# Two cross-attentions in one kernel: TensorE transposes the probabilities of two steps ago before, not after, it computes the new scores

## The chip, the cores and the metric

The kernel runs on one core of one Trainium2 chip. The metric is device time in microseconds (us) of one execution, smaller being better.

## The reference

A stack of four layers on a residual stream `x` (2 x 256 rows, 512 wide) with a context `ctx` (2 x 512 rows, 512 wide). Each layer is a cross-attention and a feed-forward part, each with its own gate:

```
x = x + tanh(g_xattn[0]) * L0_xattn(layernorm(x), ctx)
x = x + tanh(g_ffn[0])   * L0_ffn(layernorm(x))
x = x + tanh(g_xattn[1]) * L1_xattn(layernorm(x), ctx)
x = x + tanh(g_ffn[1])   * L1_ffn(layernorm(x))
...                          # layers 2 and 3: other attentions and MLPs
```

The first two attentions are the ones that the change touches. Both are grouped-query attentions whose keys and values come from the context followed by the rows themselves (512 + 256 = 768 keys for each of the 2 batches):

```
hidden = concat([ctx, x_normed])                 # 768 keys
q = x_normed @ Wq ; k = hidden @ Wk ; v = hidden @ Wv
attn = softmax(q k^T / sqrt(head_dim)) ; out = (attn v) @ Wo
# L0: 32 heads, 4 key/value heads, head_dim 128;  L1: 16 heads, 4 key/value heads, head_dim 96
```

## The kernel before, in words

One program with five engine streams, written by hand and held together by semaphores. The functions `att_pe`, `att_act`, `att_dve`, `att_pool` and `att_sp` are called once for each of the first two attentions (`A0`, then `A1`). A trip `it` runs over the 4 key/value heads, so `head(it, ...)` is executed 4 times for `A0` and 4 times for `A1`: 8 trips in all. Inside a trip the queries of all heads of the group are cut into items of 128 rows: 4 items a head, so 32 items a trip in `A0` (8 heads) and 16 in `A1` (4 heads).

A trip is a software pipeline over steps `n` (items + 4 of them). In step `n` the engines do, each in its own program order:

- TensorE (PE): the scores of item `n` (L611, 6 matmuls: queries times 768 keys, in a high and a low part of each factor), into banks 0-1 or 2-3 by the parity of `n`; now and then an output product `inner` (L576, 3 matmuls); the turn, that is the transposing of the probabilities of item `m = n - 2` (L625, 6 transposes), into banks 4 and 5; half of a product of probabilities and values of the items four and three back (L637, 9 matmuls); and a last job `job` in bank 7: a query projection of a later head ("Q", L569, 12 matmuls) or an output product of an earlier one ("O", L576, 3 matmuls).
- VectorE (DVE): the row maxima of item `n` (L813); the add of an `inner` output product (L763); every fourth step a reciprocal (L819); the remainder of the turned probabilities of item `n - 2` (L824: what the rounded copy leaves of them, read from banks 4 and 5); in odd steps the remainder of an output (L830); in steps with n % 4 = 1 a piece of the quantising of later weights (L778 to L800); the add or remainder of the `job` (L763, L767).
- ScalarE (ACT): the rounded copy of the turned probabilities of item `n - 2` (L715, read from banks 4 and 5), then the exponentials of item `n` (L722), in odd steps an output copy (L728), and the copy of a query projection (L693).

The jobs follow a fixed table (`A.steps`): a Q in steps 1, 5, 9, ... while heads are left; an O in steps 6, 7 and 8 of the first head, 10, 11 and 12 of the second, and so on, with the head's fourth O as `inner` in step 9, 13, ... Steps 2 to 4 have no job. So in the middle of a trip one step in four (n % 4 = 1) is long, with an inner O and a Q, and three are short, with one O each.

What the turn waits for: `exps` of its own item (`m + 1`), and `pT` of the item before (`m`), which DVE counts up when L824 has read banks 4 and 5, since there is one pair of banks for the turned probabilities. What the scores wait for: `exps` of item `n - 2`, whose banks they overwrite. GpSimd (POOL) splits weights into parts and SyncE (SP) issues the loads; neither is named in the change.

Of the kernel before, what the change touches and what calls it, by code (L numbers as in the profile page):

```python
# [21 lines left out]
P = 128  # L22
# [7 lines left out]
VT = S // P  # L30
# [100 lines left out]
def build(nc, t, out):  # L131
    with ExitStack() as ctx:
        sems = {}

        def sem(name):
            if name not in sems:
                sems[name] = ctx.enter_context(nc.semaphore(name))
            return sems[name]

        def sb(name, shape, dt=F32, scope=ctx):  # L140
            return scope.enter_context(nc.sbuf_tensor(name, shape, dt))

        ps = ctx.enter_context(nc.psum_tensor("ps", [P, 8, 512], F32))
# [3 lines left out]
        def bank(b, n=512, p=P):  # L147
            return ps[0:p, b, 0:n]


        ident = sb("ident", [P, P])
# [19 lines left out]
        with ExitStack() as grp:  # L171
# [7 lines left out]
            prob = sb("prob", [P, 3, S], F32, grp)  # L179
            pT = sb("pT", [P, 2, 2, VT, ROWS // B], F32R, grp)  # L180
# [246 lines left out]
        def credits(engine, name, A):  # L427
            for n, by in credit.items():
                if by == name and A is A0:
                    engine.sem_inc(sem(f"att_{n}"), 1)  # L430
# [109 lines left out]
        def att_pe(pe, A, u):  # L540
            s = {n: sem(f"att_{n}") for n in att_per(A)}
            hd = A.hd
            credits(pe, "tensor", A)
            def project(w, it, c, b):

                for k in range(KT):
                    for wp, xp in PAIRS:
                        rhs = ctxT[:, xp, k, c * CTX:(c + 1) * CTX] if c < B else xT[:, xp, k, :]
                        last = nc.tensor.matmul(bank(b, 512, hd), wkv[:, w, wp, k * hd:(k + 1) * hd], rhs,  # L549
                                                start=(k == 0 and (wp, xp) == PAIRS[0]),  # L550
                                                stop=(k == KT - 1 and (wp, xp) == PAIRS[-1]))
                last.then_inc(s["kv_full"], 1)

            def keys(it, c):
                if c == 0:
                    pe.wait_ge(s["split"], at(it, A, "split", 1))
                    pe.wait_ge(s["kv"], at(it, A, "kv", 0))
                project(0, it, c, c)

            def work(it, job, b=7):  # L560
                kind, h, r = job
                if b == 7:

                    pe.wait_ge(s["w"], at(it, A, "w", A.place[job] - 1))
                if kind == "Q":
                    pe.wait_ge(s["split"], at(it, A, "split", A.split["q", h]))
                    for k in range(KT):
                        for wp, xp in PAIRS:
                            last = nc.tensor.matmul(bank(b, 512, hd), wq[:, h % 2, wp, k * hd:(k + 1) * hd],  # L569
                                                    xT[:, xp, k, :], start=(k == 0 and (wp, xp) == PAIRS[0]),  # L570
                                                    stop=(k == KT - 1 and (wp, xp) == PAIRS[-1]))
                else:
                    pe.wait_ge(s["split"], at(it, A, "split", A.split["o", h]))
                    pe.wait_ge(s["oT"], at(it, A, "oT", 2 * h + r // 2 + 1))
                    for op, wp in PAIRS:
                        last = nc.tensor.matmul(bank(b), oT[0:hd, h % 2, op, r * P:(r + 1) * P],  # L576
                                                wo[0:hd, h % 2, wp, :], start=(op, wp) == PAIRS[0],
                                                stop=(op, wp) == PAIRS[-1])
                last.then_inc(s["w_full"], 1)

            def values(it):

                pe.wait_ge(s["split"], at(it, A, "split", 2))
                for c in range(3):
                    pe.wait_ge(s["kv"], at(it, A, "kv", c + 1))
                    project(1, it, c, c)
                work(it, ("Q", 0, 0))

                for c in range(3):
                    pe.wait_ge(s["kv_hi"], at(it, A, "kv_hi", 3 + c + 1))  # L590
                    for j in range(4):
                        last = nc.tensor.transpose(ps[:, 4 + c, j * hd:(j + 1) * hd],
                                                   vturn[0:hd, c, j * P:(j + 1) * P], ident[0:hd, 0:hd])
                    last.then_inc(s["kv_full"], 1)

            def head(it, ahead):
                def wait(name, n):
                    pe.wait_ge(s[name], at(it, A, name, n))

                for n, inner, job in A.steps:  # L600
                    if n < A.items:
                        h, r = divmod(n, RT)
                        b = r // 2
                        if r == 0:
                            wait("w", A.place["Q", h, 0])
                        if n >= 2:
                            wait("exps", n - 1)
                        sc = ps[:, 2 * (n % 2):2 * (n % 2) + 2, :].rearrange("p a c -> p (a c)")
                        for lo, hi in ((0, 512), (512, S)):
                            for qp, kp in PAIRS:  # L610
                                last = nc.tensor.matmul(sc[:, lo:hi], qT[0:hd, h % 2, qp, r * P:(r + 1) * P],  # L611
                                                        kT[0:hd, kp, b, lo:hi], start=(qp, kp) == PAIRS[0],
                                                        stop=(qp, kp) == PAIRS[-1])
                        last.then_inc(s["scores"], 1)
                    if inner:
                        work(it, inner)
                    if 2 <= n < A.items + 2:
                        m = n - 2
                        wait("exps", m + 1)
                        if m == 0:  # L620
                            wait("kv", 6)
                        if m >= 1:
                            wait("pT", m)
                        for j in range(VT):
                            last = nc.tensor.transpose(ps[:, 4 + j // 3, (j % 3) * P:(j % 3 + 1) * P],  # L625
                                                       prob[:, m % 3, j * P:(j + 1) * P], ident[:])
                        last.then_inc(s["turned"], 1)
                    if n >= 4:
                        q, second = divmod(n - 4, 2)
                        b = q % B  # L630
                        if not second:
                            wait("pT", 2 * q + 2)
                            if q >= 1:
                                wait("oT", q)
                        for j in range(3 * second, 3 * second + 3):
                            for vp, pp in PAIRS:
                                last = nc.tensor.matmul(bank(6, 256, hd), vv[:, vp, b * VT + j, 0:hd],  # L637
                                                        pT[:, q % 2, pp, j, :],
                                                        start=(j == 0 and (vp, pp) == PAIRS[0]),
                                                        stop=(j == VT - 1 and (vp, pp) == PAIRS[-1]))  # L640
                        if second:
                            last.then_inc(s["pv"], 1)
                    if job:
                        work(it, job)
                    if ahead and A.items <= n < A.items + 3:
                        keys(it + 1, n - A.items)
                for job in A.tail:
                    work(it, job, TAIL_BANKS[job[2]])
                if ahead:
                    values(it + 1)  # L650

            if A is A0:
                pe.wait_ge(sem("ctx_split"), 1)
                keys(0, 0)
                turn_pe(pe, u)
                pe.wait_ge(sem("ctx_split"), 2)
                keys(0, 1)
            else:
                keys(0, 0)
                keys(0, 1)  # L660
                turn_pe(pe, u)
            pe.wait_ge(sem("xT_lo"), (u // 2 + 1) * RT)
            keys(0, 2)
            values(0)
            with pe.Fori(0, A.kv - 1) as it:
                head(it, True)
            head(A.kv - 1, False)

        def kv_dst(A, part, c):
# [1372 lines left out]
```

## Time and profile before

| | |
|---|---|
| three runs | 1490.13, 1492.81, 1494.40 us; median 1492.81 |
| the profiled execution | 1491.04 us in all, span of its instructions 1489.3 us |
| mean granted TensorE clock | 0.969 of full speed |
| busy share of the span | PE 92%, weight loads of PE 72%, DVE 65%, ACT 40%, POOL 31% |

The profile's span goes from the first instruction to the last; 1.7 us of the execution lie outside. The first attention's steps lie between about 44 and 650 us of the span, the second's between about 730 and 1060 us. In the profile a group of matmuls is shown with the time of its first start; the start of the next group on the same engine says how long it kept the engine.

### The profile page before, as it was taken

What the parts mean: (1) busy time and instruction counts of PE and PEld (TensorE: products, weight loads), DVE (VectorE), ACT (ScalarE), POOL (GpSimd) and SP (SyncE); (2) the same over time, 40 slices, a digit from 0 to 9 for tenths busy, and PEclk for the clock granted to TensorE, in tenths of its full rate; (3) what the DMA queues carried; (4) which work ended last, traced back from release to release, by engine and by line L of the source; (5) the groups of instructions that cost most, each with busy time, mean ns of one, the idle gap of its engine ahead of it and who ended that gap; (6) DMA issues with size and microseconds to landing.
All of it is one profiled execution on the core that took longest, in us unless ns stands there. A gap on an engine that the chain in (4) does not pass through costs nothing.

```text
span 1489.3 us, 22423 instructions
## 1 busy us (share of the span) xinstructions
PE 1369.5 (92%) x8021; PEld 1073.0 (72%) x8027; DVE 965.4 (65%) x1394; ACT 599.4 (40%) x1037; POOL 467.3 (31%) x357
## 2 busy tenths in 40 slices
PE   5999989998999999989899999999689999899765
PEld 4898879887889888854687887878665444577422
DVE  3778657874878478853584865746655773463697
ACT  2544434443444344420443534434325677122111
POOL 2361445153434334421242243530232002144100
PEclk9999999999999999999999999999888999999878
DMA  5210112011110211021002011110230000561000
GB/s 184 57 40 22 61 45 61 28 61 44 36 47 22 68 57 47 8 78 37 27 1 65 21 53 32 32 38 9 72 96 1 1 2 1 139 163 44 0 0 29
DMA packets 54335, 68.13 MB, mean 46 GB/s; under 512 B 26416, under 2 KB 34896, under 8 KB 54240
## 3 DMA queue, kind: packets, MB, share of 16 engines
q1 hardware_dynamic: 54240, 66.84, 14.9%
q8 instruction: 62, 1.02, 0.3%
q14 instruction: 33, 0.27, 0.1%
HBM read 57.13 MB, written 5.37 MB: 42 GB/s over the span
## 4 chain that ended last, share of the span: by engine, by line
PE 80%; DVE 12%; issue 3%; ACT 3%; DMA 1%; POOL 0%; SPq 0%; DVEq 0%; POOLq 0%; ACTq 0%
PE ps L637 12%; PE ps L611 11%; PE ps L549 9%; PE ps L625 9%; PE ps L576 8%; PE ps L569 8%; PE ps L1502 4%; PE ps L1133 3%; PE ps L1159 3%; PE ps L1515 2%; DVE pT L824 2%; PE ps L1115 1%; ACT pT L715 1%; PE ps L1144 1%; PE ps L882 1%
## 5 line engine op out<-in xcount | busy, mean ns | idle before, releaser
L715 ACT ACTIVATE pT<-ps 128x768 fp32r<-128x768 f32 x192 | 156.0, 812 | 291.8 <-PE ps L625 291.8
L637 PE MATMUL ps<-pT,vv 128*128 128x256 f32 (+1 forms) x1728 | 249.7, 289 | 2.5 <-DVE oT L830 2.5
L824 DVE TENSOR_TENSOR pT<-ps,pT 128x768 fp32r<-128x768 f32 x192 | 183.7, 957 | 92.9 <-ACT pT L715 92.5
L611 PE MATMUL ps<-kT,qT 128*128 128x512 f32 (+3 forms) x1152 | 233.0, 339 | 4.0 <-DVE qT L767 2.6
L611 PEld LDWEIGHTS ps<-kT,qT 128*128 128x128 f32 (+1 forms) x1152 | 198.9, 188 | 43.5 <-DVE qT L767 4.2
L637 PEld LDWEIGHTS ps<-pT,vv 128*128 128x128 f32 (+1 forms) x1728 | 215.5, 180 | 4.3 <-DVE pT L824 2.9
L813 DVE TENSOR_REDUCE nmax<-ps 128x1 f32<-128x768 f32 x192 | 182.2, 951 | 23.0 <-PE ps L611 20.1
L722 ACT ACTIVATE prob<-ps,nmax 128x768 f32<-128x768 f32 x192 | 172.2, 897 | 30.2 <-DVE nmax L813 30.0
L625 PE MATMUL ps<-ident,prob 128*128 128x128 f32 x1152 | 158.7, 274 | 19.2 <-DVE pT L824 19.2
L576 PE MATMUL ps<-wo,oT 128*128 128x512 f32 (+1 forms) x576 | 163.5, 399 | 4.3 <-DVE qT L767 2.6
L625 PEld LDWEIGHTS ps<-ident,prob 128*128 128x128 f32 x1152 | 130.8, 140 | 31.6 <-ACT prob L722 17.8
L763 DVE SCALAR_TENSOR_TENSOR x<-ps,rden,x 128x512 f32<-128x512 f32 x192 | 143.2, 746 | 7.5 <-PE ps L576 2.6
L569 PE MATMUL ps<-xT,wq 128*128 128x512 f32 (+1 forms) x576 | 142.1, 395 | 0.0
L529 POOL TENSOR_TENSOR wo<-raw,one 128x512 fp32r<-128x512 f32 (+1 forms) x48 | 50.0, 1041 | 275.1 <-PE ps L576 275.1
L529 POOL TENSOR_TENSOR wq<-raw,one 128x512 fp32r<-128x512 f32 (+1 forms) x48 | 46.6, 971 | 255.9 <-PE ps L569 141.5
L569 PEld LDWEIGHTS ps<-xT,wq 128*128 128x128 f32 (+1 forms) x576 | 100.6, 179 | 27.0
L549 PE MATMUL ps<-ctxT,wkv 128*128 128x512 f32 (+1 forms) x384 | 95.0, 401 | 16.6 <-POOL wkv L532 15.0
L576 PEld LDWEIGHTS ps<-wo,oT 128*128 128x128 f32 (+1 forms) x576 | 97.0, 189 | 17.0 <-POOL wq L532 2.7
L1348 DVE TENSOR_REDUCE qrow<-ps 128x1 f32<-128x512 f32 x128 | 83.3, 687 | 36.9 <-PE ps L1133 35.7
L767 DVE SCALAR_TENSOR_TENSOR qT<-ps,qT 128x512 fp32r<-128x512 f32 (+1 forms) x48 | 33.0, 687 | 103.1 <-ACT qT L693 101.8
L1442 POOL TENSOR_TENSOR f2w<-f2raw,f2w 128x1024 fp32r<-128x1024 f32 (+1 forms) x22 | 43.1, 1963 | 178.5 <-ACT f2w L1546 177.4
L549 PEld LDWEIGHTS ps<-ctxT,wkv 128*128 128x128 f32 (+1 forms) x384 | 68.2, 179 | 37.8 <-issue 15.5
(224 smaller groups left out, 1869.2 us busy)
## 6 DMA issues: line engine op xcount, KB each, us to landing
f2raw<-in_f_w SPq DMA_DIRECT2D x11, 776.0 KB, 4.5
w3in<-in_m_w SPq DMA_DIRECT2D x11, 768.0 KB, 4.5
raw<-in_l_wq SPq DMA_DIRECT2D x32, 256.0 KB, 2.8
raw<-in_l_wo SPq DMA_DIRECT2D x32, 256.0 KB, 2.6
raw<-in_l_wq SPq DMA_DIRECT2D x16, 192.0 KB, 2.4
raw<-in_l_wo SPq DMA_DIRECT2D x16, 192.0 KB, 2.4
w3gu<-w3o SPq DMA_DIRECT2D x11, 256.0 KB, 2.6
ctxraw<-in_ctxT SPq DMA_DIRECT2D x2, 1024.0 KB, 7.6
```

Of the source, the lines that this page charges most:

```text
L529: nc.gpsimd.tensor_tensor(dst[:, HI], src, one[0:src.shape[0], :].to_broadcast(src.shape), ALU.mult).then_inc(s["split_hi"], 1)
L549: last = nc.tensor.matmul(bank(b, 512, hd), wkv[:, w, wp, k * hd:(k + 1) * hd], rhs, start=(k == 0 and (wp, xp) == PAIRS[0]), stop=(k == K ...
L569: last = nc.tensor.matmul(bank(b, 512, hd), wq[:, h % 2, wp, k * hd:(k + 1) * hd], xT[:, xp, k, :], start=(k == 0 and (wp, xp) == PAIRS[0] ...
L576: last = nc.tensor.matmul(bank(b), oT[0:hd, h % 2, op, r * P:(r + 1) * P], wo[0:hd, h % 2, wp, :], start=(op, wp) == PAIRS[0], stop=(op, w ...
L611: last = nc.tensor.matmul(sc[:, lo:hi], qT[0:hd, h % 2, qp, r * P:(r + 1) * P], kT[0:hd, kp, b, lo:hi], start=(qp, kp) == PAIRS[0], stop=( ...
L625: last = nc.tensor.transpose(ps[:, 4 + j // 3, (j % 3) * P:(j % 3 + 1) * P], prob[:, m % 3, j * P:(j + 1) * P], ident[:])
L637: last = nc.tensor.matmul(bank(6, 256, hd), vv[:, vp, b * VT + j, 0:hd], pT[:, q % 2, pp, j, :], start=(j == 0 and (vp, pp) == PAIRS[0]), ...
L715: nc.scalar.activation(turned_p(m, HI), ps[:, 4:6, 0:S // 2].rearrange("p a (j c) -> p a j c", j=3), ACT.Copy).then_inc(s["pT_hi"], 1)
L722: nc.scalar.activation(prob[:, n % 3, :], sc[:, 0:S], ACT.Exp, bias=nmax[:, n:n + 1], accum_out=rsum[:, n:n + 1]).then_inc(s["exps"], 1)
L763: nc.vector.scalar_tensor_tensor(x[:, r, :], bank(b), rden[:, RT * h + r:RT * h + r + 1], x[:, r, :], ALU.mult, ALU.add).then_inc(s["w"], 1)
L813: nc.vector.tensor_reduce(nmax[:, n:n + 1], sc[:, 0:S], AX.X, ALU.max, negate=True).then_inc(s["nmax"], 1)
L824: nc.vector.tensor_tensor(to, ps[:, 4:6, 0:S // 2].rearrange("p a (j c) -> p a j c", j=3), hi, ALU.subtract).then_inc(s["pT"], 1)
```

## The change

In every step of `head` in `att_pe` the block of the turn (its three waits, its 6 transposes and its semaphore) is moved up, in front of the block of the scores. No instruction is added, removed or changed, and no other engine's program is touched. In a step PE now does: turn of item `n - 2`, scores of item `n`, inner O, product with the values, job.

```diff
                 for n, inner, job in A.steps:
+                    if 2 <= n < A.items + 2:
+                        m = n - 2
+                        wait("exps", m + 1)
+                        if m == 0:
+                            wait("kv", 6)
+                        if m >= 1:
+                            wait("pT", m)
+                        for j in range(VT):
+                            last = nc.tensor.transpose(ps[:, 4 + j // 3, (j % 3) * P:(j % 3 + 1) * P],
+                                                       prob[:, m % 3, j * P:(j + 1) * P], ident[:])
+                        last.then_inc(s["turned"], 1)
                     if n < A.items:
                         h, r = divmod(n, RT)
                         b = r // 2
...
                         last.then_inc(s["scores"], 1)
                     if inner:
                         work(it, inner)
-                    if 2 <= n < A.items + 2:
-                        m = n - 2
-                        wait("exps", m + 1)
-                        if m == 0:
-                            wait("kv", 6)
-                        if m >= 1:
-                            wait("pT", m)
-                        for j in range(VT):
-                            last = nc.tensor.transpose(ps[:, 4 + j // 3, (j % 3) * P:(j % 3 + 1) * P],
-                                                       prob[:, m % 3, j * P:(j + 1) * P], ident[:])
-                        last.then_inc(s["turned"], 1)
                     if n >= 4:
```

## Rows read from the trace of the kernel before

**Rows 1.** The page: busy time, share of the span and instructions of each engine.
```profile
PE 1369.5 (92%) x8021; PEld 1073.0 (72%) x8027; DVE 965.4 (65%) x1394; ACT 599.4 (40%) x1037; POOL 467.3 (31%) x357
```

**Rows 2.** The page: the chain that ended last, share of the span by engine.
```profile
PE 80%; DVE 12%; issue 3%; ACT 3%; DMA 1%; POOL 0%; SPq 0%; DVEq 0%; POOLq 0%; ACTq 0%
```

**Rows 3.** The page: groups, out<-in, count | busy, mean ns | idle before, its ender.
```profile
L824 DVE TENSOR_TENSOR pT<-ps,pT 128x768 fp32r<-128x768 f32 x192 | 183.7, 957 | 92.9 <-ACT pT L715 92.5
...
L763 DVE SCALAR_TENSOR_TENSOR x<-ps,rden,x 128x512 f32<-128x512 f32 x192 | 143.2, 746 | 7.5 <-PE ps L576 2.6
```

**Rows 4.** The waits: who waited for whom, us in total, times, longest.
```profile
PE ps L625 <- DVE pT L824: 19.2, 24, 2.4
```

**Rows 5.** Timeline, two short steps of `A0`: start, duration, engine, line, [idle before].
```profile
228.97 1.21 PE L611 MATMUL ps<-kT,qT 128*128 128x512 f32 x6
...
230.02 0.82 PE L625 MATMUL ps<-ident,prob 128*128 128x128 f32 x6
230.41 0.95 DVE L813 TENSOR_REDUCE nmax<-ps 128x1 f32<-128x768 f32 x1
...
230.59 1.31 PE L637 MATMUL ps<-pT,vv 128*128 128x256 f32 x9
...
231.27 0.17 DVE L819 RECIPROCAL rden<-rsum 128x4 f32<-128x4 f32 x1
...
231.74 0.86 PE L576 MATMUL ps<-wo,oT 128*128 128x512 f32 x3
...
232.44 1.20 PE L611 MATMUL ps<-kT,qT 128*128 128x512 f32 x6
...
233.48 0.93 PE L576 MATMUL ps<-wo,oT 128*128 128x512 f32 x3
233.68 0.96 DVE L813 TENSOR_REDUCE nmax<-ps 128x1 f32<-128x768 f32 x1 [0.29 <-PE ps L611]
```

**Rows 6.** Timeline, steps 2 to 4 of the fourth trip of `A0`, PE and DVE.
```profile
523.58 0.94 DVE L813 TENSOR_REDUCE nmax<-ps 128x1 f32<-128x768 f32 x1
...
524.45 0.94 DVE L824 TENSOR_TENSOR pT<-ps,pT 128x768 fp32r<-128x768 f32 x1
...
525.53 0.85 PE L625 MATMUL ps<-ident,prob 128*128 128x128 f32 x6 [0.98 <-DVE pT L824]
...
526.13 1.29 PE L611 MATMUL ps<-kT,qT 128*128 128x512 f32 x6
...
528.36 0.85 PE L625 MATMUL ps<-ident,prob 128*128 128x128 f32 x6 [0.94 <-DVE pT L824]
...
532.96 2.96 PE L569 MATMUL ps<-xT,wq 128*128 128x512 f32 x12
```

**Rows 7.** Timeline of PE, the last steps of `A0` (29 to 32) in its fourth trip.
```profile
630.54 1.20 PE L611 MATMUL ps<-kT,qT 128*128 128x512 f32 x6
...
634.06 1.21 PE L611 MATMUL ps<-kT,qT 128*128 128x512 f32 x6
...
641.45 0.85 PE L625 MATMUL ps<-ident,prob 128*128 128x128 f32 x6 [0.22 <-DVE pT L824]
```

**Rows 8.** Timeline of PE, two short steps of `A1`.
```profile
840.39 1.20 PE L611 MATMUL ps<-kT,qT 96*128 96x512 f32 x6
...
843.82 1.20 PE L611 MATMUL ps<-kT,qT 96*128 96x512 f32 x6
```

**Rows 9.** Timeline of PE, start of the second trip of `A0`.
```profile
211.75 1.99 PE L611 MATMUL ps<-kT,qT 128*128 128x512 f32 x6
213.97 1.51 PE L625 MATMUL ps<-ident,prob 128*128 128x128 f32 x6 [0.24 <-DVE pT L824]
215.13 1.48 PE L637 MATMUL ps<-pT,vv 128*128 128x256 f32 x9
```

**Rows 10.** Windows: stretch, us and count by engine, granted clock, DMA share, GB/s.
```profile
213.00:216.00 3.00, 2.76 (x16) 2.50 (x15) 1.82 (x3) 1.20 (x3) 0.00 (x0) 0.59 0.03 12
...
652.00:656.00 4.00, 1.99 (x9) 1.31 (x7) 3.79 (x10) 0.00 (x0) 0.73 (x2) 1.00 0.02 4
```

## The prediction

> **What bounds the kernel now.** I read the page first, its busy shares and its chain, then the waits, then the timeline of a few steps. PE is busy for 92% of the span [rows 1] and makes 80% of the chain that ended last [rows 2], so each microsecond that PE loses inside a trip is lost to the end. In the two attentions PE hardly waits: the largest entry that the change touches is the turn (L625) waiting for DVE's remainder of the turn before (L824), 19.2 us in 24 waits [rows 4], that is three for each of the 8 trips: two near its start [rows 6] and one near its end [rows 7]. Everything between runs without a gap. The slack is on the other side: DVE sits idle for 92.5 us in front of L824, waiting for ACT's copy of the turned probabilities [rows 3].
>
> A short step of `A0` takes 3.47 us (scores at 228.97, next scores at 232.44), and that is PE's own work and nothing else: scores 1.05, turn 0.57, product with the values 1.15, output product 0.70 [rows 5]. In `A1` it takes 3.43 us [rows 8].
>
> **What the change does to the order.** PE's program is cyclic, so between one turn and the next it issues the same groups as before, and the work of PE as a sum is unchanged. What changes is what stands between the turn and the scores. There is one pair of banks for the turned probabilities, so turn `m` waits until DVE has done remainder `m - 1`. DVE's own program is not touched: in step `n` it does the maxima of item `n` first, and only then the remainder of item `n - 2`. Before, the scores of step `n` were computed ahead of turn `n - 2`: when the turn was done, DVE was already through the maxima or nearly so. After, the turn comes first, but DVE still can't do its remainder until it has done the maxima of scores that PE only now begins. From turn to turn there is a chain, which after the change goes
>
> turn, scores, maxima, remainder, next turn.
>
> **Its length, link by link.** A turn that had to wait keeps PE for 0.60 us until the next group starts (525.53 to 526.13) [rows 6], one that did not for 0.57 (230.02 to 230.59) [rows 5]. From the start of the scores to the start of the maxima, with DVE waiting for them, 1.24 us (232.44 to 233.68) [rows 5]. From the start of the maxima to the start of the remainder directly behind them 0.87 us (523.58 to 524.45) [rows 6]. The remainder itself takes 0.96 us [rows 3]. From its end to the start of the waiting turn 0.14 us (524.45 + 0.94 = 525.39, turn at 525.53) [rows 6]. Sum: 0.60 + 1.24 + 0.87 + 0.96 + 0.14 = 3.81 us. In a step with n % 4 = 0 the reciprocal stands between maxima and remainder: it takes 0.17 us [rows 5], with its start I count 0.20, so 4.01 us. In the first short step behind a long one the turn has not waited: 3.78 us.
>
> ACT is not in this chain: its copy starts when the turn's 0.6 to 0.85 us are over and is done about 1.7 us behind the turn's start, while the maxima end at 0.60 + 1.24 + 0.87 = 2.71 us. So the 92.5 us of DVE before L824 mostly go away, and reappear as idle time before the maxima (L813), where they are no use.
>
> So the chain is longer than PE's own work in a short step, and PE must wait for the difference in every one of them. In a long step (n % 4 = 1, with a Q of 2.8 us) it is covered: there PE has over 6 us of work of its own. Behind a Q, DVE also has its remainder of the new queries to do before the maxima; the turn now lies between, so this is no later than the scores.
>
> **The sum.**
> - Short steps in threes. Each three of `A0` costs (3.78 - 3.47) + (3.81 - 3.47) + (4.01 - 3.47) = 0.31 + 0.34 + 0.54 = 1.19 us. There are 6 such threes in a trip (steps 6 to 8 up to 26 to 28) and 4 trips: 24 x 1.19 = 28.6. In `A1`, with 3.43: 0.35 + 0.38 + 0.58 = 1.31, 2 threes in a trip: 8 x 1.31 = 10.5.
> - The start of a trip, steps 3 to 5, without output products. Before, from the turn of step 3 to the Q of step 5 it takes 532.96 - 525.53 = 7.43 us, with a wait of 0.94 in it [rows 6]. The turn of step 3 stays where it is: it waits for the remainder of item 0, and DVE comes to that late because of the quantising and the queries' remainder in front of maxima 2, with the turn moved or not. After it come 3.81 (step 3), 4.01 (step 4) and turn, scores and product 0.60 + 1.05 + 1.15 = 2.80: 10.62 us, 3.19 more. 8 trips: 25.5.
> - Step 29 (`A1`: 13), which has an inner output product and no Q. Before: 634.06 - 630.54 = 3.52 [rows 7]. After: DVE has the add of the inner product between maxima and remainder, 0.75 us [rows 3], 0.67 apart with the same overlap of 0.07 as between maxima and remainder. 3.81 + 0.67 = 4.48, so 0.96 more; 8 x 0.96 = 7.7.
> - The last two steps with scores (30, 31). Before, 641.45 - 634.06 = 7.39, with the wait of 0.22 in it [rows 7]; after 2 x 3.81 = 7.62: 0.23 more, 8 x 0.23 = 1.8. Later steps have no scores, and their order doesn't change.
>
> 28.6 + 10.5 + 25.5 + 7.7 + 1.8 = 74.1 us, from 136 steps that the chain sets (23 in a trip of `A0`, 11 in one of `A1`). No DMA, no instruction of another engine is added or moved past another, and SP and POOL are far from the path: later loads only get more time. On the profiled execution's own 1491.0 us this makes 1565.1; the median of the three runs shown is 1.8 us above it, so 1567.
>
> **Bounds of it.** The trace of before has no step in this order, so each link is taken from another place. With the least value of each (0.57 for the turn, 0.94 for the remainder) the chain is 3.76; with no overlap on DVE at all (0.95 for the maxima) 3.89. I take 3.81, as its links are each read where somebody really waited. Minus 0.05 to plus 0.08 over 136 steps is -7 to +11 us; another 0.05 either way on the step from the last score matmul to the maxima, which I have only from places where another group follows the scores, 7 us. The forecast's own range is 1553 to 1585.
>
> One rule of the Trainium skill would size a link otherwise. In the rows two DVE operations start 0.87 us apart where the first is recorded with 0.94 [rows 6]. The page "VectorE: DVE Perf Modes", section "The DRAIN you can't avoid", says that the next operation doesn't start until the pipeline is empty; by that the chain would be at least 0.07 longer, 136 x 0.07 = 10 us and 1577 in all, but here the row contradicts it, and I keep the row.
>
> **The rivals.**
> - *The clock falls at the trips' starts.* After the change PE is idle for about half of steps 3 and 4 (work 1.65 of 3.81, 2.80 of 4.01), and a little in step 5's surroundings. In the second trip of `A0` the granted clock did fall, to 0.59 of full speed over three microseconds [rows 10], after a wait of 2.4 us; scores then take 1.98 us (213.97 - 211.75 less the 0.24 of waiting) in place of 1.05 and the turn 1.16 (215.13 - 213.97) in place of 0.57 [rows 9], 1.5 us more for both. Two such steps in all 8 trips: 24 us, 1591. Against it: three of four trips of `A0` had the same kind of start and kept the clock, and at 652 to 656 us PE was busy half of the time at full clock [rows 10]. Some of it may happen.
> - *It falls all along.* PE would now have a gap of about 0.3 us in every short step. If the clock swung down for a good half of the 136 steps, 70 x 1.5 = 105 us: 1672. Nothing in the rows has such a pattern of small regular gaps; full clock through half-idle stretches speaks against it. By the Trainium skill ("TensorE: Matmul & The Clock Gate", section "A second HAM failure mode: psum-queue depth-cycling") frequent small idle times between groups of matmuls can make the clock gate swing between its two levels; no row here shows it.
> - *Half of the chain is covered.* If DVE starts the maxima earlier than I read, or PE holds less than 3.47 us of work in the new order, and the chain came to 3.6 us, the short steps would cost half, the rest somewhat less: about 74 - 136 x 0.2 = 47 us, 1540. The links are too well seen for this.
> - *No change.* The order is only rotated, PE's sum of work is the same and PE is the bound. This holds if the chain stays under PE's 3.43 to 3.47 us. It needs an error of 0.35 us in five links that sum to 3.81. 1493.
> - *Faster.* The turn comes 1.05 us earlier relative to the scores, ACT's copy too, DVE no longer idles for it (92.5 us), and PE's 19.2 us of waits for L824 [rows 4] go: 1474. It decides for this side if the remainder can be done ahead of the maxima. DVE's program order forbids that.
>
> **Chances.** Forecast 0.76; clock at the starts 0.10; clock all along 0.02; half covered 0.06; no change 0.03; faster 0.03. The range, 1545 to 1592, takes the forecast with its bounds and the case of the starts; outside are the last four and a small part of the first. A measurement can tell about 0.3% (4.5 us) from no change: faster 0.03, same 0.03, slower 0.94.
>
> **What the profile after would show.** Span about 1563, PE's busy time near 1370 and so near 88%. PE L625 waiting for DVE L824 not 24 times but in nearly each short step, 140 to 180 times, 90 us or so in all. In a short step turns 3.8 us apart, 4.0 where the reciprocal stands; in a long step unchanged. L824 directly behind L813 (0.87 apart) with hardly any wait for ACT, and DVE idle before L813 for PE L611 much more than before. At the start of a trip turns at 3.8 and 4.0 and a wait of PE of some 2 us before each. The prediction is wrong in mechanism if L824 still waits for ACT, if the turns are 3.5 us apart, or if the groups of PE themselves become longer at a lower clock.

## The result, and the profile after

The changed kernel takes 1584.52 us (median of 4 runs, 1583.25 to 1587.12), the kernel before 1491.47 us (4 runs, 1488.20 to 1494.40): a ratio of 1.0638, 95% interval 1.0600 to 1.0677. It is 93 us slower. The forecast was 1567 us, in a range of 1545 to 1592; direction and mechanism were right, the size was 74 of 93 us, and the measured time lies in the range, near its upper end.

The page of the changed kernel: busy time by engine, then the chain that ended last by engine, then three of its groups, which answer to [rows 1 to 3].

```profile
PE 1407.3 (89%) x8027; PEld 1066.0 (67%) x8027; DVE 953.0 (60%) x1394; ACT 617.9 (39%) x1037; POOL 467.6 (30%) x357
...
PE 68%; DVE 19%; issue 9%; ACT 2%; DMA 1%; POOL 0%; SPq 0%; DVEq 0%; POOLq 0%; ACTq 0%
...
L813 DVE TENSOR_REDUCE nmax<-ps 128x1 f32<-128x768 f32 x192 | 183.4, 957 | 202.2 <-PE ps L622 199.1
...
L609 PE MATMUL ps<-ident,prob 128*128 128x128 f32 x1152 | 163.5, 279 | 79.9 <-DVE pT L824 62.7
...
L824 DVE TENSOR_TENSOR pT<-ps,pT 128x768 fp32r<-128x768 f32 x192 | 181.2, 944 | 1.9 <-ACT pT L715 1.9
```

The scores are L622 now and the turn L609. PE's part of the chain has fallen from 80 to 68%, DVE's has risen from 12 to 19%. DVE's idle time has moved: the 92.5 us in front of the remainder [rows 3] are 1.9, and in front of the maxima there are 199 us of waiting for scores, where the kernel before had 20.

The waits of PE in the changed kernel (us in total, times, longest), to be read beside [rows 4]:

```profile
PE ps L609 <- DVE pT L824: 62.7, 104, 4.3
PE ps L609 <- ACT prob L722: 17.0, 40, 1.0
```

Together 80 us in 144 waits, against 19.2 in 24. The second row is the same wait as the first: the turn waits for both semaphores, and where the reciprocal stands in the step the profile names the wrong one (the exponentials were long done, the remainder ended 0.15 us ahead of the turn, as the next rows show).

The timeline of three short steps in a row (a "three") in the second trip of the first attention, PE and DVE (the first turn stands behind a long step):

```profile
240.20 0.82 PE L609 MATMUL ps<-ident,prob 128*128 128x128 f32 x6
...
244.07 0.84 PE L609 MATMUL ps<-ident,prob 128*128 128x128 f32 x6 [0.24 <-DVE pT L824]
244.67 1.29 PE L622 MATMUL ps<-kT,qT 128*128 128x512 f32 x6
...
245.80 1.24 PE L637 MATMUL ps<-pT,vv 128*128 128x256 f32 x9
246.00 0.96 DVE L813 TENSOR_REDUCE nmax<-ps 128x1 f32<-128x768 f32 x1 [1.20 <-PE ps L622]
246.88 0.95 DVE L824 TENSOR_TENSOR pT<-ps,pT 128x768 fp32r<-128x768 f32 x1
...
247.97 0.84 PE L609 MATMUL ps<-ident,prob 128*128 128x128 f32 x6 [0.23 <-DVE pT L824]
...
250.86 0.93 DVE L824 TENSOR_TENSOR pT<-ps,pT 128x768 fp32r<-128x768 f32 x1
...
251.94 0.84 PE L609 MATMUL ps<-ident,prob 128*128 128x128 f32 x6 [0.30 <-ACT prob L722]
```

This is the chain of the prediction, and it can be read off link by link between 244.07 and 247.97: turn 0.60, scores to maxima 1.33, maxima to remainder 0.88, remainder 0.95, 0.14 to the next turn; 3.90 us. The turns lie 3.87, 3.90 and 3.97 us apart; the forecast was 3.78, 3.81 and 4.01.

### The profile page after: what moved, and what is told of

It is laid out like the page before. It is cut to its first block, busy times and chain, and to the rows that moved or that the text cites. A ratio compares the mean times of both kernels' runs of the same rounds, so it can differ in the third digit from the quotient of the medians.

```text
span 1581.5 us, 22459 instructions
## 1 busy us (share of the span) xinstructions
PE 1407.3 (89%) x8027; PEld 1066.0 (67%) x8027; DVE 953.0 (60%) x1394; ACT 617.9 (39%) x1037; POOL 467.6 (30%) x357
## 4 chain that ended last, share of the span: by engine, by line
PE 68%; DVE 19%; issue 9%; ACT 2%; DMA 1%; POOL 0%; SPq 0%; DVEq 0%; POOLq 0%; ACTq 0%
PE ps L622 12%; PE ps L609 10%; PE ps L549 8%; PE ps L569 8%; DVE pT L824 6%; PE ps L637 4%; DVE nmax L813 4%; PE ps L1502 4%; PE ps L576 3%; PE ps L1133 2%; PE ps L1159 2%; PE ps L1515 2%; PE ps L1115 1%; PE ps L1144 1%; PE ps L882 1%
## 5 line engine op out<-in xcount | busy, mean ns | idle before, releaser
L813 DVE TENSOR_REDUCE nmax<-ps 128x1 f32<-128x768 f32 x192 | 183.4, 957 | 202.2 <-PE ps L622 199.1
L622 PE MATMUL ps<-kT,qT 128*128 128x512 f32 (+3 forms) x1152 | 251.6, 356 | 3.4 <-DVE qT L767 3.2
L637 PE MATMUL ps<-pT,vv 128*128 128x256 f32 (+1 forms) x1728 | 237.3, 282 | 2.2 <-DVE oT L830 2.1
L609 PE MATMUL ps<-ident,prob 128*128 128x128 f32 x1152 | 163.5, 279 | 79.9 <-DVE pT L824 62.7
L637 PEld LDWEIGHTS ps<-pT,vv 128*128 128x128 f32 (+1 forms) x1728 | 220.7, 182 | 9.4 <-DVE pT L824 2.5
L609 PEld LDWEIGHTS ps<-ident,prob 128*128 128x128 f32 x1152 | 127.5, 142 | 139.4 <-issue 92.9
L622 PEld LDWEIGHTS ps<-kT,qT 128*128 128x128 f32 (+1 forms) x1152 | 192.0, 193 | 30.8 <-DVE qT L767 5.1
L824 DVE TENSOR_TENSOR pT<-ps,pT 128x768 fp32r<-128x768 f32 x192 | 181.2, 944 | 1.9 <-ACT pT L715 1.9
L569 PE MATMUL ps<-xT,wq 128*128 128x512 f32 (+1 forms) x576 | 144.4, 399 | 0.4
L569 PEld LDWEIGHTS ps<-xT,wq 128*128 128x128 f32 (+1 forms) x576 | 100.2, 179 | 32.0 <-issue 4.0
```

The lines of the kernel that those rows point to most:

```text
L813: nc.vector.tensor_reduce(nmax[:, n:n + 1], sc[:, 0:S], AX.X, ALU.max, negate=True).then_inc(s["nmax"], 1)
L824: nc.vector.tensor_tensor(to, ps[:, 4:6, 0:S // 2].rearrange("p a (j c) -> p a j c", j=3), hi, ALU.subtract).then_inc(s["pT"], 1)
```

## The experiments

All runs of a batch shared the chip with runs of the kernel before, whose medians were 1491.42, 1491.30 and 1492.82 us. Turn-to-turn distances below are read from the timeline of PE of each profiled execution.

**e1: VectorE does the remainder first.**

```diff
                 for n, inner, job in A.steps:          # att_dve
+                    if 2 <= n < A.items + 2:
+                        ...                            # the remainder of item n - 2
                     if n < A.items:
                         ...                            # the maxima of item n
```

> The changed kernel, with one thing more: in each step VectorE does the remainder of the turned probabilities (item n-2) before the maxima (item n), so that the remainder no longer waits for scores that come behind the turn. Theory A (the loss is the chain turn, scores, maxima, remainder, next turn): the chain becomes turn, ScalarE copy, remainder, next turn, about 2.85 us, shorter than the 3.48 us of TensorE's own work in a short step; short steps fall from 3.90 back to about 3.48, and the time to 1485 to 1502 us. Theory B (the loss is in TensorE itself: its groups or its clock are worse in the new order, transposes ahead of scores): VectorE's order doesn't matter and the time stays at 1560 us or more.

Measured: 1565.85 us, ratio 1.0511 (1.0479 to 1.0542). Theory A's time was missed by far, and by the time alone theory B (1560 us or more) would have been right. The steps decide against B: the first two short steps of a three are 3.48 and 3.47 us, as A has it, so the chain did go. The loss came back elsewhere. Long steps took 7.74 us in place of 6.58, the third short step 3.84. The waits of PE in e1:

```profile
PE ps L569 <- DVE x L763: 28.4, 24, 1.3
PE ps L609 <- DVE pT L814: 27.8, 23, 2.6
PE ps L637 <- DVE oT L830: 22.7, 33, 1.4
```

The query projection (L569) waits for DVE to empty bank 7, and the product with the values (L637) for the remainder of the output. Neither was in the theory. The timeline of e1 around such a long step:

```profile
250.87 0.85 PE L576 MATMUL ps<-wo,oT 128*128 128x512 f32 x3
251.38 0.96 DVE L814 TENSOR_TENSOR pT<-ps,pT 128x768 fp32r<-128x768 f32 x1 [1.04 <-ACT pT L715]
...
252.26 0.95 DVE L819 TENSOR_REDUCE nmax<-ps 128x1 f32<-128x768 f32 x1
253.12 0.74 DVE L763 SCALAR_TENSOR_TENSOR x<-ps,rden,x 128x512 f32<-128x512 f32 x1
...
254.00 3.06 PE L569 MATMUL ps<-xT,wq 128*128 128x512 f32 x12 [1.20 <-DVE x L763]
```

The inner output product is ready near 251.9, but DVE has remainder and maxima to do before it adds it. With the maxima the exponentials are late too, and behind them on ACT the output's copy. So e1 showed in its short steps that the chain is real, and in its time that the remedy moves the wait; that these two waits are what it lost was tested in e9.

**e2: the product with the values in between turn and scores.** The block of L637 is moved in front of the block of the scores in the changed kernel; nothing else.

> The changed kernel with the product with the values moved in between turn and scores (order of a step: turn, product, scores, inner output, job). TensorE's sum of work is the same. Theory A: the product's 1.07 us come into the chain of each short step from the fourth on, of steps 29 to 31 (13 to 15 in the second attention) and of step 4: 22 steps in a trip of the first attention, 10 in one of the second, 128 in all, 1.07 each: 137 us more than the changed kernel, about 1720 us, more if the clock falls in the longer waits. Short steps 4.97 us. Theory B (TensorE's own work): same time as the changed kernel, 1575 to 1595 us.

Measured: 1777.31 us (2 runs). Theory B is out: the same work of PE in another order costs 193 us more. The short steps are 4.95 and 4.98 us, as theory A has it. The third one, 5.26 in place of 5.04, and the long one, 7.65 in place of 6.58, were not expected: the product now also delays the add of the output products, and PE waits for it 25.7 us in 24 times in front of the Q. 24 x 1.07 and 32 x 0.22 explain 33 of the 57 us by which the time is above 1720. I left the rest (half-clock spells among it) unresolved.

**e3: shorter maxima.** The maxima are taken over 256 of the 768 scores.

```diff
-                        nc.vector.tensor_reduce(nmax[:, n:n + 1], sc[:, 0:S], AX.X, ALU.max,
+                        nc.vector.tensor_reduce(nmax[:, n:n + 1], sc[:, 0:256], AX.X, ALU.max,
```

> The changed kernel, with the row maxima taken over the first 256 of the 768 scores only (the exponentials are then taken relative to that smaller maximum, which leaves the softmax the same as long as nothing overflows). The operation should fall from 0.95 to about 0.42 us. Theory A: the chain falls by 0.53 us to 3.37, under TensorE's 3.48, so short steps cost nothing more than before the change; what is left is the starts (about 2.2 us in each of 8 trips), step 29 or 13 (0.5 us) and long steps: 1513 us (1503 to 1522). Theory B: 1575 to 1590 us, since VectorE's maxima are on nobody's path.

Measured: 1500.39 us (7 runs, 1496.47 to 1514.41), ratio 1.0072 (1.0042 to 1.0102). That is 3 us below the expected range, and 13 below the time expected. The profiled execution took 1509.97 us, near the slow end of the seven, so the trace does not show what the quicker ones saved. Maxima in e3 and two short steps:

```profile
L813 DVE TENSOR_REDUCE nmax<-ps x192: 407/424/427, 47.4 to 1067.4; 128x1 f32<-128x256 f32 x192
...
244.20 0.82 PE L609 MATMUL ps<-ident,prob 128*128 128x128 f32 x6
...
247.69 0.82 PE L609 MATMUL ps<-ident,prob 128*128 128x128 f32 x6
...
251.18 0.82 PE L609 MATMUL ps<-ident,prob 128*128 128x128 f32 x6
```

0.53 us less in one DVE operation took 84 of the 93 us away. The turns are 3.49 us apart and have no wait in front of them any more: this is PE's own work in the new order, 0.02 more than in the old [rows 5]. At the starts, where PE has less to do, the steps are 3.32 to 3.37 us in the six trips that keep the full clock there: the chain, as forecast 3.37.

**e7: the same cut in the kernel before**, as a control.

> Control for e3: the kernel before with the maxima over the first 256 of 768 scores only. In the old order the maxima are beside TensorE's work, so 0.53 us less in each of 192 of them buys next to nothing: 1484 to 1493 us. If this gains 50 us or more, e3 says nothing about the chain, but only that VectorE's time counts everywhere.

Measured: 1485.00 us, ratio 0.9956 (0.9938 to 0.9975). 6 us where e3 had 84. So the 0.53 us of DVE are worth next to nothing in the old order, and the 84 us of e3 belong to the new one. Of the 4.5 us between the profiled executions (1486.54 and 1491.04) 3.0 lie behind the last turn of the attentions, where the program is the same.

**e4: the remainder first in the kernel before.**

> The kernel before the change (scores ahead of the turn), with VectorE's remainder ahead of its maxima. Theory A: in the old order neither is on the path; the remainder comes up to 0.87 us earlier at the starts of the trips, where TensorE waits for it: 1486 to 1493 us, no difference that can be told or a little less. A rival: VectorE then idles until the turn's copy is there before it starts the maxima, and the exponentials come late enough to hold the scores two steps on: 1500 us or more.

Measured: 1680.84 us, ratio 1.1274 (1.1240 to 1.1308). This was the worst miss of my theory, and the rival was right with its sign. The wait that the rival names, scores for the exponentials, is only 7.8 us in 8 times. The two largest waits of PE in the attentions in e4:

```profile
PE ps L637 <- DVE oT L830: 68.2, 50, 1.9
PE ps L569 <- DVE x L763: 57.9, 24, 2.4
```

They are the two waits of e1, larger: 126 of the 189 us. I read the difference from e1 as this: in the old order the turn, and so the remainder and what DVE now does behind it, comes 1 us later in the step. No run tests that by itself. What the runs do show is that the old kernel's two orders fit together: scores ahead of the turn on PE, maxima ahead of the remainder on DVE.

**e5 and e6: the change in parts.** In e5 the turn is moved in steps 2 to 5 alone (`2 <= n < A.items + 2 and n < 6` at the new place, the rest at the old), in e6 in all other steps.

> The kernel before with the turn moved ahead of the scores in steps 2 to 5 of each trip alone; from step 6 on the old order. If the sum by parts holds, only the starts pay: 3.25 us in each of 8 trips and some 8 us more for the half clock in trips 2 to 4 of the first attention, 33 us in all: 1524 us (1514 to 1530). On the clock: if the long waits of the starts are what lets it fall, the spells of half clock at the starts of trips 2 to 4 are here as in the changed kernel. If the small gaps of the short steps matter, they are not.

> The complement: the old order in steps 2 to 5, the turn moved from step 6 on. By the parts: short steps in threes 43, long steps 5, step 29 or 13 8, last steps 3, less the wait of step 18 that goes (4), and 2 between the trips: 58 us, 1549 us (1543 to 1556), and no more half clock inside the trips than the kernel before shows (one spell at the start of a trip). A rival in which the parts do not add (the long waits of the start and the later steps share a cause): this alone costs over 75 us or e5 and e6 together are off the changed kernel's 93 us by more than 10.

Measured: e5 1524.00 us, ratio 1.0206 (1.0181 to 1.0231), 33 us; e6 1545.53 us, ratio 1.0356 (1.0333 to 1.0378), 54 us. Their sum is 87 of 93 us, so the parts add. Windows of the clock (us, busy by engine, then the granted clock, DMA share, GB/s), first the changed kernel, then e5, then e6:

```profile
219.00:225.00 6.00, 2.16 (x16) 1.85 (x16) 5.43 (x7) 2.81 (x6) 4.22 (x4) 1.00 0.28 65
225.00:232.00 7.00, 4.99 (x22) 4.26 (x21) 1.82 (x2) 2.61 (x4) 0.00 (x0) 0.55 0.05 19
399.00:406.00 7.00, 4.99 (x21) 4.24 (x21) 1.82 (x2) 2.61 (x4) 0.00 (x0) 0.56 0.08 31
570.00:580.00 10.00, 7.97 (x33) 7.15 (x33) 3.33 (x5) 3.17 (x6) 1.12 (x1) 0.53 0.17 49
```

```profile
215.00:225.00 10.00, 7.92 (x32) 6.78 (x30) 3.71 (x5) 3.58 (x6) 0.00 (x0) 0.51 0.05 20
539.00:549.00 10.00, 7.99 (x32) 7.15 (x33) 3.29 (x5) 3.10 (x6) 1.08 (x1) 0.52 0.14 45
942.00:952.00 10.00, 7.99 (x33) 6.96 (x31) 3.55 (x5) 3.35 (x5) 0.47 (x1) 0.51 0.08 20
```

```profile
221.00:225.00 4.00, 3.36 (x12) 2.90 (x13) 2.28 (x4) 2.22 (x5) 0.00 (x0) 0.57 0.23 66
...
430.00:580.00 150.00, 142.42 (x859) 120.37 (x857) 98.22 (x135) 64.68 (x116) 53.44 (x40) 1.00 0.15 46
```

With the moved starts there are long spells of half clock, 7 to 10 us each, at the starts of three trips; without them e6 has short ones, of the kind of [rows 10]. Which trips are hit differs, and so my expectation for e5 held in part only: trips 2 and 4 of the first attention have a long spell, trip 3 a short one (0.57 of full speed over 379 to 383 us), and the third long one lies in the second attention, where the changed kernel had none. And 150 us of e6 with a gap of PE in front of nearly every short step's turn stay at full clock.

**e8: a version in the old order.** The three small operations on the block maxima of the later weights are moved behind the remainder of the next step.

```diff
+                    if n % RT == 2 and A.quantises(it) and n // RT in A.amax_at:
+                        block_exponents(A.tile(it, A.amax_at[n // RT]))   # lines 780 to 785 of before
                     if n % RT == 1 and A.quantises(it):
                         if n // RT in A.amax_at:
                             block_maxima(A.tile(it, A.amax_at[n // RT]))  # now the reduction alone
```

> The kernel before (old order), with the three small operations on the block maxima of the later weights (lines 781 to 785, which took up to 3 us together beside GpSimd) moved from the steps with n % 4 = 1 behind the remainder of the next step. Theory: at the starts of trips 2 and 3 of the first attention they hold the queries' remainder, the maxima and the remainder that the second turn waits for (wait 2.4 us in place of 1.0), and in step 18 they hold TensorE by 0.9 us. Both go: 3 + 4 = 7 us less, 1484 to 1487 us, 0.3 to 0.5% faster than the kernel before. Rival: the small operations then hold the maxima of step 3 or 19 and nothing is gained: 1489 to 1494 us.

Measured: 1482.49 us (6 runs), ratio 0.9950 (0.9932 to 0.9968): 9 us faster than the kernel before, and 2 us below the range expected. The start of the second trip on PE, to be read beside [rows 9]:

```profile
208.46 0.84 PE L625 MATMUL ps<-ident,prob 128*128 128x128 f32 x6 [0.94 <-ACT prob L722]
209.06 1.29 PE L611 MATMUL ps<-kT,qT 128*128 128x512 f32 x6
211.61 0.85 PE L625 MATMUL ps<-ident,prob 128*128 128x128 f32 x6 [1.26 <-DVE pT L826]
```

The second turn of the trip waits 0.94 in place of 2.38 us; the third waits 0.3 more, since the small operations now hold the maxima of step 3. The 4.43 us of step 18 are 3.46. The half clock at the start of trip 2 is gone as well. Not all of the 9 us come from there. Between the two profiled executions (8.9 us) the stretch from the first to the last turn of the attentions gives 4.7, the time ahead of it 0.5, and 3.7 lie behind the last turn, where no instruction was changed and the mean granted clock was 0.92 in place of 0.90. So the move itself is worth some 5 us in these traces; the rest may be how the clock fell.

**e9: e1 with its two new waits taken away.** DVE: remainder, add of the inner product, maxima. ACT, in odd steps: the output's copy ahead of the exponentials.

> e1 (turn ahead of the scores, remainder ahead of the maxima) with its two new waits taken away by order alone: VectorE adds the inner output product ahead of the maxima, ScalarE copies the output ahead of the exponentials. If those two waits are what e1 lost (28.4 us of TensorE before the query projection, waiting for the add, and 22.7 us before the product with the values, waiting for the output's remainder), it comes to about 1515 us (1505 to 1527), still slower than the kernel before, because copy, remainder, maxima, exponentials and the next copy now form a ring of 3.58 us, which the starts show (3.58 in place of 2.83). If it comes to under 1495, the moved turn costs nothing once the other engines follow it; if it stays over 1550, e1's loss lies elsewhere.

Measured: 1511.35 us, ratio 1.0133 (1.0097 to 1.0169). 54 us came back, where the two waits of e1 were 51: they account for it. What is left is visible in the turns of a trip: 3.58 and 3.59 us at the start (before the change 2.83), 6.67 in the long steps (6.33), 3.48 in the short ones. With the turn ahead no order of the other engines that I tried reaches the kernel before.

## Why the prediction was right, and where it was short

The mechanism held. That the turn comes to stand behind the maxima of scores which PE has only just begun is shown by e3 and e7 (shorten the maxima: 84 us in the new order, 6 in the old) and by e2 (lengthen the way to them: 193 us more). The sum by its terms, measured between the points that the prediction used, in both profiled executions, whose difference is 1583.25 - 1491.04 = 92.2 us:

| term | forecast | measured |
|---|---|---|
| short steps in threes | 28.6 + 10.5 = 39.1 | 24 x 1.33 + 8 x 1.41 = 43.2 |
| starts of trips | 25.5 | 32.3 (8 x 3.25 = 26.0, and 6.3 in the three trips at half clock) |
| step 29 or 13 | 7.7 | 8 x 1.04 = 8.3 |
| last two steps with scores | 1.8 | 8 x 0.41 = 3.3 |
| long steps | 0 | 5.4 |
| the stall of step 18, gone | 0 | -3.6 |
| the rest, from the last steps to the turn of step 3, and outside the trips | 0 | 3.3 |
| sum | 74.1 | 92.2 |

**The link from scores to maxima was mis-sized.** "With DVE waiting for them, 1.24 us" was read where the scores stand behind an output product. Behind a turn they take longer; the loads of their weights (PEld) in the changed kernel and, for comparison, before:

```profile
244.64 1.11 PEld L622 LDWEIGHTS ps<-kT,qT 128*128 128x128 f32 x6
```

```profile
228.75 1.22 PEld L611 LDWEIGHTS ps<-kT,qT 128*128 128x128 f32 x6
```

Before, the first load began 0.22 us ahead of the first matmul (228.75, 228.97 in [rows 5]), under the output product; now it begins 0.03 ahead (244.64, 244.67). The scores keep PE for 1.13 us in place of 1.04, and the link is 1.33. That makes the chain 3.90. It goes with the group in front: in e2, where the product with the values stands between turn and scores, the scores keep PE for 1.05 us and the link is 1.25 (medians of 78 places). Why a group takes longer there is not shown. The group's 1.29 us of busy time behind a turn could be seen before (526.13 in [rows 6]); I took that row for the length of the turn and not for that of the scores. The reciprocal costs 0.08, not 0.20.

**The clock at the starts** was priced apart, as a rival with 24 us and a chance of 1 in 10. It is not a rival but a part: it came in three of eight trips of the profiled execution and cost 6.3 us more than the kernel before had paid for its own spell. e5 and e6 show that the long spells come with the waits of the starts. Two grounds for the low chance were weaker than they looked. By "three of four trips had the same kind of start" only the third trip had as long a wait as the second (from the turn of step 2 to that of step 3 it took 4.25 and 4.27 us in these two, 2.92 and 2.85 in the first and fourth), so one of two such starts had been hit. And behind the half-idle stretch at full clock of [rows 10] the clock did fall, to 0.57 over 659 to 663 us. The other clock rival, half clock all along, did not occur: e6 shows it. The Trainium skill ("TensorE: Matmul & The Clock Gate", section "A second HAM failure mode: psum-queue depth-cycling") says that small frequent idle times can make the clock swing; the windows do not agree for this kernel, with 1.00 over 150 us of such steps.

**The long steps** were costed at nothing, "covered". They take 6.58 for 6.33 us. In the changed kernel the Q waits for the add of the inner product in them:

```profile
254.74 0.74 DVE L763 SCALAR_TENSOR_TENSOR x<-ps,rden,x 128x512 f32<-128x512 f32 x1
...
255.62 3.07 PE L569 MATMUL ps<-xT,wq 128*128 128x512 f32 x12
```

The add ends at 255.48 and the Q begins 0.14 us later, the distance of every other such wait. The add stands behind the maxima on DVE, and these stand behind scores that start 0.6 us later in the step. It is the same wait that grew to 1.20 us in e1. With the maxima cut (e3) long steps are 6.38 us, and from the product to the Q it takes 1.08 us in place of 1.24: so the wait is 0.16 of the 0.25 us, and the rest is PE's own, the longer scores among it.

**The stall of step 18** (4.43 us for 3.47 in three trips, 4.19 in one, with PE waiting for DVE's queries' remainder) I had not counted as something to be gained; the later maxima absorb it. e8 takes it away in the old order.

**The rivals.** No change, faster and half covered are all out by e2 and e3. The rule of the Trainium skill ("VectorE: DVE Perf Modes", section "The DRAIN you can't avoid"), by which the sum would have been 1577, does not hold for this pair: maxima and remainder start 0.88 us apart with 0.96 us recorded for the first (246.00 and 246.88). The section itself goes on to say that a next operation which is not held starts earlier; the prediction left that out. By its number 1577 would have been nearer to 1584.52 than 1567 was, but that would have been luck, since the missing time lay in the link in front of the maxima.

The expected signs were there: span, turns 3.8 to 4.0 us apart, L824 right behind L813. PE's busy time grew from 1369.5 to 1407.3 us, where it was to stay near 1370. By groups, the scores' busy time grew by 18.6 us, the turns' by 4.8, and that of the product with the values fell by 12.4; with the other groups it comes to 14.5. The other 23 us are stretches in which the records of two groups overlapped before and no longer do.

## What to carry to other kernels

Rotating the order on one engine keeps its work and changes what stands in each cycle of waits through the other engines. Before such a move, follow the loop through the fixed order of every engine it passes (here PE turn, PE scores, DVE maxima, DVE remainder) and compare its length with the work of the bounding engine in the shortest step. If the order of a second engine is changed to suit, its own loops and all shared buffers (here bank 7 and the output's copy) have to be followed too: e1 and e4 came out 74 and 189 us slower than the kernel before. Read the length of a link from a place with the same neighbour in front of it, and look at small operations that stand in front of a buffer's release: moving three of them was worth some 5 us.

## What the runs showed of the hardware that was not expected

The six matmuls of the scores, behind six 128-column transposes, took 1.13 us where behind 512-column matmuls they took 1.04, with the first weight load 0.03 in place of 0.22 us ahead of the first matmul. The granted clock fell to half (1.2 GHz of 2.4) for 7 to 10 us at three starts of the changed kernel; over the 6 us before, PE had been busy for 2.16 us (219 to 225), 1.74 (393 to 399) and 3.98 (564.5 to 570.5). Not each such start was hit: with 4.00 of 6 us busy (890 to 896) the clock stayed full. And operations of DVE on 48 columns that mostly take 0.17 to 0.24 us took 0.80 to 1.28 in some places; in the changed kernel, in a start where GpSimd was busy for 4.22 of 6 us:

```profile
221.12 0.96 DVE L783 TENSOR_SCALAR w3inv<-w3amax 128x48 uint32<-128x48 uint32 x1
222.00 0.17 DVE L785 TENSOR_SCALAR w3amax<-w3amax 128x48 uint32<-128x48 uint32 x1
```

In the traces before and after there are 24 that take 0.80 us or more, and every one of them lies beside an operation of GpSimd; but 22 of the short ones do so too. That GpSimd is the cause was not tested.
